# The last stage of a two-attention and expert layer: normalised rows by ScalarE, token sums as a column of the Gram matrix, no staging copies

## The reference, cut to what matters

```python
xn = layernorm(x)                       # x: (2, 2048, 256), no weights
x1 = xn + token_diffusion(layernorm(xn)*ln1_w+ln1_b) * gamma1   # 16 heads, softmax over 2048 tokens
a2 = layernorm(x1, eps) * ln2_w + ln2_b
qk, v = a2 @ Wqk_c, a2 @ Wv_c           # 8 groups of 32 channels
dot = einsum('bhcn,bhdn->bhcd', qk, qk) # over the 2048 tokens of a batch
attn = softmax((2*dot - q2[:,None] - q2[None,:]) / sqrt(2048) * tau_c)   # q2 = diagonal of dot
x2 = x1 + (attn @ v) @ Wo_c * gamma2
out = x + x2 + top1_expert_ffn(xn)      # 8 experts, d_ff 1024
```

## Time and profile before

| | |
|---|---|
| median of 3 runs | 1478.68 us (1476.77 to 1479.13) |
| profiled execution | 1478.41 us, its span 1476.7 us |
| mean granted clock of TensorE | 0.987 |
| busy in the span | TensorE 94%, ScalarE 72%, VectorE 27%, GpSimd 16% |
| last stage, about 1355 us to the end | 121 us |

### The profile page before, as it was taken

How to read it: one execution, slowest core, us unless ns; L and a number is a source line. 1 busy time by engine, 2 the same in 40 slices (tenths; PEclk the granted TensorE clock), 3 DMA queues, 4 the chain that set the end, 5 groups by cost and what they waited for, 6 DMA issues and landing times. The chain is left out here.

```text
span 1476.7 us, 27029 instructions
## 1 busy us (share of the span) xinstructions
PE 1391.3 (94%) x9041; PEld 663.7 (45%) x9041; DVE 403.0 (27%) x1009; ACT 1064.6 (72%) x1183; POOL 232.2 (16%) x314
## 2 busy tenths in 40 slices
PE   6997999999999999999999999999999999999978
PEld 4752222234444444444444444344444444444867
DVE  6872110011111211112111111111121111123977
ACT  4657999987777777777777777777777777775122
POOL 5210730001001000010010100100001001001870
PEclk9998999999999999999999999999999999999989
DMA  4686442724543626345454454353544645532423
GB/s 165 232 239 215 127 89 54 224 37 115 157 112 123 145 85 170 98 110 167 104 163 114 110 155 116 130 127 87 154 122 105 171 104 157 136 133 84 152 89 115
DMA packets 125321, 195.38 MB, mean 132 GB/s; under 512 B 22336, under 2 KB 91648, under 8 KB 121824
## 3 DMA queue, kind: packets, MB, share of 16 engines
q1 hardware_dynamic: 116240, 177.12, 44.0%
q0 software_dynamic: 9040, 17.71, 4.4%
HBM read 154.63 MB, written 35.95 MB: 129 GB/s over the span
## 5 line engine op out<-in xcount | busy, mean ns | idle before, releaser
L939 ACT ACTIVATE shared<-ps 128x1024 f32<-128x1024 f32 x1024 | 980.5, 1024 | 264.8 <-PE ps L1076 263.8
L1091 PE MATMUL ps<-shared,work 128*17 128x512 f32 x4096 | 505.6, 603 | 0.0
L1076 PE MATMUL ps<-mov,stat 52*128 52x512 f32 x2048 | 423.7, 465 | 51.3 <-ACT shared L939 37.4
L1076 PEld LDWEIGHTS ps<-mov,stat 52*128 52x128 f32 x2048 | 167.5, 185 | 428.4 <-ACT shared L939 402.4
L984 DVE TENSOR_SCALAR work<-ps,work 128x128 f32<-128x128 f32 x312 | 109.6, 351 | 587.2 <-PE ps L1134 572.3
L1091 PEld LDWEIGHTS ps<-shared,work 128*17 128x17 f32 x4096 | 90.1, 97 | 220.8 <-issue 199.2
L1134 PE MATMUL ps<-work,XNW 128*128 128x128 f32 x1248 | 180.7, 288 | 0.0
L1134 PEld LDWEIGHTS ps<-work,XNW 128*128 128x128 f32 x1248 | 151.0, 191 | 57.0 <-issue 57.0
L1118 PE MATMUL ps<-XNW,work 128*128 128x256 f32 x624 | 161.8, 382 | 0.0
L788 POOL DMA_DIRECT2D y_slots<-work x39 | 21.9, 562 | 701.2 <-DVE work L976 642.2
L1118 PEld LDWEIGHTS ps<-XNW,work 128*128 128x128 f32 x624 | 106.5, 191 | 12.8 <-issue 4.8
(11 more groups left out here) (170 smaller groups left out, 689.7 us busy)
## 6 DMA issues: line engine op xcount, KB each, us to landing
XNW<-in_L_ffn_W_dram SPq DMA_DIRECT2D x78, 1024.0 KB, 7.1
stat<-q_parts SPq DMA_DIRECT2D x192, 128.0 KB
mov<-q_parts SPq DMA_DIRECT2D x192, 64.0 KB
xg<-in_L_attn_x_dram SPq DMA_DIRECT2D x16, 512.0 KB, 4.9
q_parts<-XNW SPq DMA_DIRECT2D x16, 512.0 KB, 5.8
x_slots<-work SPq DMA_DIRECT2D x1, 4992.0 KB, 16.4
early<-x_slots SPq DMA_DIRECT2D x39, 128.0 KB, 2.2
early<-in_L_ffn_b_dram SPq DMA_DIRECT2D x39, 128.0 KB, 8.1
```

Of the source, the lines that this page charges most:

```text
L939: nc.scalar.activation(probs[:, s % DEEP, half * 1024:(half + 1) * 1024], ps[:, 2 * half:2 * half + 2].rearrange("p a b -> p (a b)"), ACT. ...
L1076: last = nc.tensor.matmul(ps[:, 2 * half + r], stat[rows, hh, m * P:(m + 1) * P], mov[rows, hh, half * 512:(half + 1) * 512], start=True, ...
L1091: last = nc.tensor.matmul(ps[32 * j:32 * j + VW, AV], Vh[:, hh, m], probs[:, s % DEEP, j * 512:(j + 1) * 512], start=(m == 0), stop=(m == ...
```

## The change

1. ScalarE makes the normalised rows z = (x1 - mean)/std from `nmr` = -mean/std, a new small VectorE step behind a wait for the root. ln2_w and ln2_b are no longer applied to rows: ScalarE applies them by channel when it takes the transposed rows from PSUM.
2. The Gram matrix is that of z with a column of ones (257 columns), so the tokens' sums come with it. ln2_w is folded into `wqks` (Wqk scaled, made early); ln2_b enters by one-row products: a row bq = ln2_b·Wqk (`shift_row`), the sums turned into a row at `corner`, a rank-one product in `product_t`, a last row `trow` that VectorE finishes (`last_row`), and a rank-one product in `product_dots`.
3. `finals` read `a2T` directly; `stage_f` is gone and the loops are written out.
4. `add_expert` of groups 0 to 7 moves ahead of its `final`, and waits for its own group's gathers. The first projections no longer wait for the clearing.

```diff
-        N_LATE = 7 + CH
+        N_LATE = 5 + 2 * KC + CH
...
-                for dst, src in ((l2w, ln2_w), (l2b, ln2_b), (g1r, gamma1), (g2r, gamma2)):
+                for dst, src in ((g1r, gamma1), (g2r, gamma2)):
                     sp.dma_start(dst[:, :], src.partition_broadcast(P)).then_inc(late_loaded, 16)
+                for c in range(KC):
+                    for dst, src in ((l2w, ln2_w), (l2b, ln2_b)):
+                        sp.dma_start(dst[:, c:c + 1], src[c * P:(c + 1) * P].rearrange("(p a) -> p a", a=1)
+                                     ).then_inc(late_loaded, 16)
...
+                for c in range(KC):
+                    mark(nc.vector.tensor_scalar(wqks[:, c], wqkc[:, c], l2w[:, c:c + 1], None, ALU.mult))
...
                 def rstd(G, par):
                     pool.wait_ge(var3_ready, G + 1)
+                    at_least(pool, z2_ready, G - 1)
                     nc.gpsimd.tensor_tensor(rs1[:, par], ve1[:, par], nhalf[:, 0], ALU.pow).then_inc(rstd3_ready, 1)
                 def add_x(G, par):
-                    pool.wait_ge(a2_ready, G + 1)
+                    pool.wait_ge(z2_ready, G + 1)
...
+                def make_z2(G, par):
+                    act.wait_ge(neg_mean3_ready, G + 1)
+                    if G >= 2:
+                        act.wait_ge(ring3_ready, 2 * (G - 2) + KC)
+                    for t in range(GT):
+                        last = nc.scalar.activation(z2g[:, par, t, 0:D], XN[:, G * GT + t], ACT.Identity,
+                                                    bias=nmr[:, par, t:t + 1], scale=rs1[:, par, t:t + 1])
+                    last.then_inc(z2_ready, 1)
+                def take_a2(G):
                     for c in range(KC):
-                        act.wait_ge(ring3_ready, use_a2(G) + c + 1)
-                        nc.scalar.copy(a2T[c][:, G * GN:(G + 1) * GN], ps[:, c]).then_inc(ring3_taken, 1)
+                        act.wait_ge(ring3_ready, 2 * G + c + 1)
+                        nc.scalar.activation(a2T[c][:, G * GN:(G + 1) * GN], ps[:, c], ACT.Identity,
...
-                    bank = ps[:, 4 + b].rearrange("p (c n) -> p c n", c=KC)
-                    nc.scalar.copy(gram[:, b], bank).then_inc(gram_copied, 1)
+                    nc.scalar.copy(gz[:, b], ps[:, 4 + b, 0:2 * D - P + 2]).then_inc(gram_copied, 1)
                     act.wait_ge(corner_turned, b + 1)
-                    nc.scalar.copy(gram[:, b, 1, 0:P], bank[:, 1, 0:P]).then_inc(gram_copied, 1)
+                    nc.scalar.copy(gcorner[:, b], ps[:, T_BANK[b], 0:P])
+                    nc.scalar.copy(srow[0:1, b], ps[0:1, T_BANK[b], P:P + D]).then_inc(gram_copied, 1)
...
-                def stage_f(G, par):
-                    at_least(act, fin_ready, 2 * (G - 1))
-                    nc.scalar.copy(a2s[:, par, 0], a2T[0][:, bass.ds(G * GN, GN)])
-                    nc.scalar.copy(a2s[:, par, 1], a2T[1][:, bass.ds(G * GN, GN)]).then_inc(staged, 1)
...
+                act.wait_ge(bq_ready, 1)
+                nc.scalar.copy(bqrow[0:1], ps[0:1, D_BANK[0], 0:D]).then_inc(bq_copied, 1)
+                make_z2(0, 0)
+                make_z2(1, 1)
+                for G in range(GB - 1):
+                    take_a2(G)
+                    make_z2(G + 2, G % 2)
+                take_a2(GB - 1)
                 take_gram(0)
                 take_t(0)
-                for tt in range(3):
-                    act.wait_ge(y_stored[tt], 16 * (PAIRS - FIRST))
-                take_a2(GROUPS - 4, 0)
-                take_a2(GROUPS - 3, 1)
+                make_z2(GROUPS - 3, 1)
+                take_a2(GROUPS - 4)
+                make_z2(GROUPS - 2, 0)
+                take_a2(GROUPS - 3)
                 exp_of(0)
-                stage_f(0, 0)
-                stage_f(1, 1)
-                take_a2(GROUPS - 2, 0)
+                make_z2(GROUPS - 1, 1)
+                take_a2(GROUPS - 2)
                 take_r(0)
-                take_a2(GROUPS - 1, 1)
+                take_a2(GROUPS - 1)
                 take_gram(1)
                 take_t(1)
-                stage_f(2, 0)
                 exp_of(1)
-                stage_f(3, 1)
                 take_r(1)
...
+                def add_expert(G):
                     dve.wait_ge(x_added, G + 1)
+                    dve.wait_ge(gathered[G], 16 * GT)
...
-                def make_a2(G, par):
...
+                def make_nmr(G, par):
...
+                    at_least(dve, z2_ready, G - 1)
+                    nc.vector.scalar_tensor_tensor(nmr[:, par], mv1[:, par, :, 0], -1.0, rs1[:, par], ALU.mult, ALU.mult
+                                                   ).then_inc(neg_mean3_ready, 1)
...
+                def last_row(b):
+                    dve.wait_ge(tlast_ready, b + 1)
+                    dve.wait_ge(bq_copied, 1)
+                    nc.vector.scalar_tensor_tensor(trow[0:1, b], bqrow[0:1], float(S), ps[0:1, R_BANK[b], 0:D],
+                                                   ALU.mult, ALU.add).then_inc(trow_ready, 1)
...
-                def final(G, par):
-                    add_expert(G, par)
+                def final(G):
...
+                def x1(G):
+                    make_x1(G, G % 2)
+                    make_nmr(G, G % 2)
+                x1(0)
                 nc.vector.memset(pblk, 0.0).then_inc(blocks_cleared, 1)
-                for G in range(GB + 1):
-                    make_x1(G + 1, (G + 1) % 2)
-                    make_a2(G, G % 2)
-                make_x1(GROUPS - 2, 0)
-                make_a2(GROUPS - 3, 1)
+                for G in range(1, GB + 1):
+                    x1(G)
+                add_expert(0)
+                x1(GROUPS - 3)
+                add_expert(1)
+                x1(GROUPS - 2)
+                last_row(0)
+                add_expert(2)
                 own_dots(0)
-                make_a2(GROUPS - 2, 0)
+                x1(GROUPS - 1)
                 shifted_logits(0)
-                make_x1(GROUPS - 1, 1)
+                add_expert(3)
                 dve.wait_ge(blocks_cleared, 1)
                 probabilities(0)
-                make_a2(GROUPS - 1, 1)
                 fold(0)
-                dve.wait_ge(gathered, 16 * TILES)
-                final(0, 0)
+                last_row(1)
+                final(0)
                 own_dots(1)
-                final(1, 1)
+                add_expert(4)
+                final(1)
                 shifted_logits(1)
+                add_expert(5)
                 probabilities(1)
-                final(2, 0)
+                final(2)
                 fold(1)
-                final(3, 1)
-                with dve.Fori(GB // 2, GROUPS // 2) as it:
-                    for par in range(2):
-                        final(2 * it + par, par)
+                add_expert(6)
+                final(3)
+                add_expert(7)
+                for G in range(GB, GROUPS):
+                    final(G)
...
+                def shift_row():
+                    for c in range(KC):
+                        last = nc.tensor.matmul(ps[0:1, D_BANK[0], 0:D], l2b[:, c:c + 1], wqkc[:, c],
+                                                start=(c == 0), stop=(c == KC - 1))
+                    last.then_inc(bq_ready, 1)
...
+                    pe.wait_ge(z2_ready, G + 1)
                     bank = ps[:, 4 + G // GB]
                     for t in range(GT):
-                        nc.tensor.matmul(bank[:, 0:D], a2g[:, par, t, 0:P], a2g[:, par, t],
-                                         start=False, stop=False, skip_group_check=True)
-                        last = nc.tensor.matmul(bank[:, D + P:2 * D], a2g[:, par, t, P:D], a2g[:, par, t, P:D],
+                        z = z2g[:, G % 2, t]
+                        nc.tensor.matmul(bank[:, 0:G1], z[:, 0:P], z, start=False, stop=False, skip_group_check=True)
...
                 def corner(b):
                     pe.wait_ge(gram_copied, 2 * b + 1)
-                    nc.tensor.transpose(ps[:, 4 + b, D:D + P], gram[:, b, 0, P:D], ident[:, :]).then_inc(corner_turned, 1)
+                    nc.tensor.transpose(ps[:, T_BANK[b], 0:P], gz[:, b, P:D], ident[:, :])
+                    for c, at in enumerate((S0, S1)):
+                        last = nc.tensor.matmul(ps[0:1, T_BANK[b], (c + 1) * P:(c + 2) * P], gz[:, b, at:at + 1],
+                                                ident[:, :], start=True, stop=True)
+                    last.then_inc(corner_turned, 1)
...
                 def product_t(b):
+                    pe.wait_ge(bq_copied, 1)
                     pe.wait_ge(gram_copied, 2 * b + 2)
+                    rows = ((gz[:, b, 0:P], gcorner[:, b]), (gz[:, b, P:D], gz[:, b, G1:S1]))
                     for M in range(KC):
                         for c in range(KC):
-                            last = nc.tensor.matmul(ps[:, T_BANK[b], M * D:(M + 1) * D], gram[:, b, c, M * P:(M + 1) * P],
```

(45 more changed lines are left out.)

135 lines of the change are left out of this document (59 added, 76 removed).

## The result

| | before | after |
|---|---|---|
| median | 1478.26 us (1476.77 to 1479.13) | 1494.22 us (1493.6 to 1495.07) |
| profiled execution, its span | 1478.41, 1476.7 | 1494.67, 1493.0 |
| mean granted clock | 0.987 | 0.981 |
| first root to the end of the span | 112.8 | 130.8 |

The changed kernel is slower: ratio 1.0113, interval 1.01 to 1.0126, 16.0 us. The forecast of 1488 us is 9.7 above the kernel before's median, and the measured 1494.22 lies 0.2 us above the top of its range of 1482 to 1494. The last row of the table is the measure for all that follows: the start of GpSimd's first root (L1269; L1255 before) to the end of the span. I call it the stage. It leaves out the 1360 us ahead of it, which differ by about 3 us from one execution to the next.

The account below looks back on a forecast made before the run. GpSimd was taken to pace the stage after the attention, TensorE its end. Last addition 1472.84 + 4.0 + 1.6 = 1478.5; with the store, span 1482.3; 1.7 more, 1484.0; clock +4, 1488 us; range 1482 to 1494.

Parts of the forecast that it names:

- Start: Start of the stage after the attention: first projection no longer waits for the clearing, about 1.6 us gained, first root 1362.3.
- Groups 0 to 6: GpSimd's groups after the attention: period stays about 8.5 us, removing VectorE's passes buys nothing, root 6 at 1409.0.
- Held `nmr`: VectorE's nmr step waits while GpSimd adds x: root to nmr 3.4 us instead of 1.04.
- `nmr` first: Rival: nmr gets ahead of add_x and runs free; 1481.3 at full clock, 1484 to 1485 with the fall; chance 0.07.
- GpSimd was slowed by VectorE's passes: Rival at the gathers: without VectorE's two passes GpSimd's groups get shorter; 12 us less, 1472; chance 0.07.
- Middle and end at full clock: Group 4 to finals(0): +4.0 us; from finals(0) to finals(4): +1.6 us; 1484.0 ahead of the clock.
- its clock term: Work behind two TensorE gaps partly at half clock: +4 us together, a third of the 11.7 at most.
- the upper end of the bounds: One-row or one-column products with 256 moving columns cost the full 0.43 us; nothing would save 2.6 us.
- Both gaps: TensorE idle ahead of the first dots, 1408.8 to 1413.0 (4.2 us), and the first r, 1425.7 to 1429.6 (3.9).
- The forecast gap at the dots: TensorE waits for VectorE's last row ahead of the first dots, 1408.8 to 1413.0, 4.2 us.
- low throughout: Rival: the clock stays at half from the first gap through the second, 5.6 + 4 or more, 1494; chance 0.11.
- the gap at 1413: Kernel before: stretch with TensorE busy 1.13 of 4.50 us, followed by clock 0.51 up to 1431.5.

Follow-up runs that it names:

- e1: Changed kernel with 23 spare products that nothing reads, put into TensorE's five gaps; 1484.53 us, ratio 1.0054 to the kernel before.
- e4: Changed kernel with GpSimd's add_x behind its four gathers instead of ahead of them; 1482.96 us, ratio 1.0043 to the kernel before.
- e9: Changed kernel with eight spare products, results unused, ahead of the first dots product alone; 1491.14 us, ratio 1.0104 to the kernel before.
- e12: Changed kernel with x1 of the next group ahead of nmr, add_x behind the gathers, expert additions 3 to 5 behind the probabilities; 1481.23 us, ratio 1.0045.
- e3: Changed kernel with x1 of the next group ahead of the waiting nmr, and ScalarE's copy of r 0 ahead of the last group's rows; 1484.17 us.
- e11: Changed kernel with three spare products ahead of the second corner and one ahead of its T; 1488.46 us, ratio 1.0076 to the kernel before.
- e7: Changed kernel with e12's orders, ScalarE's Gram and corner copies ahead of the second transposed half, sum row ahead of T; ratio 0.995 to the kernel before.
- e10: Changed kernel with six spare products, results unused, ahead of the first r alone; 1488.55 us, ratio 1.0086 to the kernel before.

## Why the prediction was right or wrong, by its steps

**Start.** -1.6 forecast, first root at 1362.3; measured 1362.16, -1.75. But this point moves between executions (1358.93 to 1362.16 in the changed kernel and the eight variants of e1 to e4 and e9 to e12), so the agreement is in part luck.

**Groups 0 to 6.** Held `nmr`, steady 8.5 us groups, GpSimd as the pacemaker: right (2.31, 8.4 to 8.5, root 6 0.8 us early). The rivals "`nmr` first" and "GpSimd was slowed by VectorE's passes" fell with these rows. The passes were worth nothing there, as forecast.

**Middle and end at full clock.** e1 is the test. The forecast without its clock term had a stage of 120.0 us (1362.3 to 1482.3); e1 has 121.4. First root to `finals(0)`: 80.6 forecast, 81.8 measured (1359.27 to 1441.04). `finals(0)` to `finals(4)`: 20.7 forecast, 21.3 measured. The second r waited 1.24 us, 1.9 forecast. The small miss is in T with its rank-one rows and the sum row: 3.5 us forecast (2.6 + 0.87), 4.30 measured at full clock, 0.8 too little. Half of it lies in the new rows (0.62 each for the rank-one products instead of 0.43) and the other half in T's full products, which stand 0.53 us apart here instead of 0.43. So the upper end of the bounds, the full price for products of one row or one column, was right, and even short.

**The clock, the step that failed.** "I take +4 for both together, a third of the 11.7 at most." Both gaps came, and both lowered the clock: 2.9 behind the dots and 1.6 at M, 4.5 together. That the +4 comes so near is luck, since no row stood behind the third. What was missing is a third stretch, T, sum row and `finals(0)` of the second batch, 4.8 us. The prediction has the waits there in its sum (two activations, Gram copy, corner copies), each one short, and it asked only whether a wait of 4 us lowers the clock. The kernel before has like waits ahead of its second corner and T, 1.22 and 0.35 us, and keeps its clock behind them, so its trace spoke against it. Why the changed kernel doesn't is open (e3 and e4 above). The forecast gap at the dots was shorter than thought (1.50 us of waiting, 4.2 forecast), since the dots started 1.0 us earlier than forecast and Gram 4 ended at 1410.5 instead of 1408.8 (`project(6)` had itself run at half clock, 5.16 us, behind a wait of 2.49), and the clock fell nevertheless. In e11, where `project(6)` ran at full clock, the wait was 2.96. The rival "low throughout", at 1494, has the right time for another reason: the clock was back at 1.00 between the stretches.

The step rested on a reading of the kernel before that was too short. The prediction says that its waits "each" end with VectorE, from the two rows, and puts the low stretch of the earlier trace rows (1424.5 to 1431.5) down to the gap at 1413. The same view of its waits has these rows too:

```profile
PE ps L1560 <- DVE late L1440: 3.2, 2, 2.9
...
PE ps L1525 <- ACT XNW L1292: 1.2, 1, 1.2
```

The 2.9 us are the wait at its first r, which ends at 1424.9. The trace has two low stretches, one behind each wait, with the clock back at 1.00 from 1422 to 1424 between them. So one stretch did not run "from the first gap through the second" there, a wait of 2.9 us was followed by one too, and ScalarE's waits at the second corner were never weighed.

In all, forecast of the profiled execution +9.6 = -1.6 (start) + 7.2 (stage, 112.8 to 120.0) + 4 (clock). Measured +16.3 in the span = -1.75 (start) + 8.6 (stage at full clock, 112.8 to 121.4 in e1) + 9.4 (clock). The forecast was 1.4 too little for the work and 5.4 too little for the clock.

## What to carry to other kernels

A change that takes work away from one engine can leave TensorE with more or longer short waits, and the work behind them can run at half clock, as here. List all the waits of TensorE in the new order, not only the longest, and whichever engine ends them. Which of them will lower the clock can't be read off one profile: the runs here give no rule for it. The spare products are a cheap test: if more work makes a kernel faster and the granted clock goes to 1.00, as in e1, the loss was clock. Here the change cost 1.1% in the order in which it came. With its lists in the order of e7 it is 0.5% faster than the kernel before in its old order.

## What the hardware showed that I had not expected

- The same waits lowered the clock in one kernel and not in another. The 1.47 and 0.70 us at the second corner were followed by a clock of 0.54 over 11.2 us in the changed kernel, and by 1.00 in e10, where only a wait ten us earlier was filled. By what rule is open.
- The clock also differs between executions where the code doesn't. The lists of e9 and e10 are the same up to `project(6)` and behind it, as far as the first dots. TensorE waited 2.45 us in both, and `project(6)` ran at full clock in e9 and mostly at half in e10:

```profile
1394.99 3.69 PE L1529 MATMUL ps<-wo,V 128*128 128x256 f32 x16 [2.45 <-DVE XNW L1386]
```
```profile
1396.09 5.16 PE L1529 MATMUL ps<-wo,V 128*128 128x256 f32 x16 [2.45 <-DVE XNW L1386]
```

- VectorE's small one-input step L1397 (TENSOR_SCALAR, 128x4) took 2.65 us (e4) and 3.03 us (e12) instead of 0.17 while GpSimd added x. I had counted only instructions with two SBUF inputs as held. The kernel before has it already: its L1378 took 2.07 us, until the `add_x` of 1394.78 was through (row below). The Trainium skill, page "SBUF — State Buffer", section "Who interferes with whom", says that an instruction with one SBUF input contends with GpSimd only in a 2-port mode, which a tensor_scalar can enter; the held rows agree with that exception, though no row here shows the mode. In e12 it had begun at 1412.81, 0.65 us ahead of that addition's start at 1413.46, beside a gather.

```profile
1395.09 2.07 DVE L1378 TENSOR_SCALAR vv<-mv 128x4 f32<-128x4 f32 x1
```

- Four expert additions held by two GpSimd additions in a row took 6.74 us instead of 1.66.
